# Second layer's sums through two wide buffers, attention's weights prepared earlier, last output block by block

## The reference, cut to what matters

```python
xn = layernorm(x)                                   # over the last axis
def rfs(v):                                         # 256 random features
    return exp(xis) / 16 * exp(v @ (xis[:, None] * proj).T - 0.5 * sum(v * v) * xis**2)
s = rfs(xn) @ rfs(input_weights).T                  # 256 features, 256 outputs
h = silu(xn @ w1.T * w1_s) * (xn @ w2.T * w2_s)     # 256 -> 1024
h = gelu(h @ h1.T * h1_s)                           # 1024 -> 1024
h = gelu(h @ h2.T * h2_s)                           # 1024 -> 1024
out = x + s * silu(h @ w3.T * w3_s)                 # 1024 -> 256
```

## Time and profile before

| | us |
|---|---|
| median of 3 runs | 1387.88 (1386.78 to 1389.29) |
| the profiled execution's own time | 1389.23 |
| its span, first to last instruction | 1387.4 |
| PE busy | 1328.2 (96%) |
| DVE busy | 963.5 (69%) |
| ACT busy | 784.9 (57%) |
| POOL busy | 595.2 (43%) |
| DMA, mean rate over the span | 140 GB/s |

### The profile page before, as it was taken

One profiled execution on the slowest core, in us unless ns is written; L12 is line 12 of the kernel. 1 busy time (PEld: TensorE's weight loads), 2 busy tenths in 40 slices (PEclk: granted clock), 3 DMA queues, 4 the chain that ended last, 5 costly groups with the idle time before them and its releaser, 6 DMA issues.

```text
span 1387.4 us, 17297 instructions
## 1 busy us (share of the span) xinstructions
PE 1328.2 (96%) x6684; PEld 1133.9 (82%) x6684; DVE 963.5 (69%) x1233; ACT 784.9 (57%) x1065; POOL 595.2 (43%) x624
## 2 busy tenths in 40 slices
PE   5999099999999999999999999999999999999996
PEld 4888089888888889888898888988888888988886
DVE  6677086787977787688866777566776666666574
ACT  4556065566655656555655566555665565655663
POOL 4545598889888888899982000000000000000000
PEclk9999599999999999999999999999999999999999
DMA  9975443254522554234432444224442244313441
GB/s 363 336 269 195 133 150 99 96 175 160 167 95 87 168 171 130 99 126 160 163 109 70 152 139 140 89 74 137 152 137 77 76 138 151 107 46 122 138 150 48
DMA packets 88647, 193.89 MB, mean 140 GB/s; under 512 B 10608, under 2 KB 12400, under 8 KB 87920
## 3 DMA queue, kind: packets, MB, share of 16 engines
q1 hardware_dynamic: 79088, 160.22, 34.7%
q0 software_dynamic: 9472, 32.51, 6.8%
HBM read 167.53 MB, written 34.60 MB: 146 GB/s over the span
## 4 chain that ended last, share of the span: by engine, by line
PE 86%; DMA 7%; POOL 5%; issue 1%; DVE 0%; SPq 0%; ACT 0%; POOLq 0%; DVEq 0%
PE ps L205 67%; PE ps L208 18%; DMA ry<-in_h 4%; POOL ry L490 3%; DMA hs<-ry 1%; PE ps L220 1%; DMA s<-in_h 1%; DMA quad<-in_w 1%; POOL quad L490 1%; POOL hs L80 0%; POOL ry L80 0%; POOL s L490 0%; DVE ry L188 0%; DMA ry<-in_x 0%; DMA ring<-hs 0%
## 5 line engine op out<-in xcount | busy, mean ns | idle before, releaser
L205 PE MATMUL ps<-split,ring 128*128 128x512 f32 x2800 | 764.8, 390 | 31.7 <-DMA ring<-hs 31.7
L205 PEld LDWEIGHTS ps<-split,ring 128*128 128x128 f32 x2800 | 526.2, 188 | 141.9 <-DMA ring<-hs 32.8
L188 DVE TENSOR_TENSOR split<-quad,split 128x1024 fp32r<-128x1024 f32 x256 | 330.3, 1300 | 179.5 <-ACT split L184 179.1
L184 ACT ACTIVATE split<-quad 128x1024 fp32r<-128x1024 f32 x256 | 266.0, 1052 | 88.3 <-PE ps L208 70.6
L208 PE MATMUL ps<-split,ring 128*128 128x512 f32 x784 | 305.2, 389 | 0.0
L205 PE MATMUL ps<-xT,w 128*128 128x512 f32 x768 | 219.5, 394 | 4.7 <-DVE xT L188 2.5
L527 POOL TENSOR_TENSOR cube<-cube,seen 128x256 f32<-128x256 f32 x176 | 190.7, 1084 | 13.8
L184 ACT ACTIVATE quad<-quad,cols 128x512 f32<-128x512 f32 (+1 forms) x194 | 138.9, 718 | 91.9 <-DVE quad L188 91.8
L184 ACT ACTIVATE quad<-ps 128x512 f32<-128x512 f32 x192 | 112.5, 596 | 135.0 <-PE ps L208 134.9
L205 PEld LDWEIGHTS ps<-xT,w 128*128 128x128 f32 x768 | 145.1, 190 | 35.2 <-DVE xT L188 2.9
L208 PEld LDWEIGHTS ps<-split,ring 128*128 128x128 f32 x784 | 147.3, 188 | 30.6
(11 more groups left out here) (94 smaller groups left out, 1160.9 us busy)
## 6 DMA issues: line engine op xcount, KB each, us to landing
ring<-hs SPq DMA_DIRECT2D x448, 256.0 KB, 3.4
xin<-in_x SPq DMA_DIRECT2D x16, 512.0 KB, 5.5
s_h<-s SPq DMA_DIRECT2D x16, 512.0 KB, 2.9
seen<-in_h POOLq DMA_DIRECT2D x64, 128.0 KB, 2.9
ry<-in_x SPq DMA_DIRECT2D x16, 512.0 KB, 4.6
out<-ry SPq DMA_DIRECT2D x16, 512.0 KB, 2.7
...
```

The costliest lines, as they stand in the source:

```text
L184: return act.mark(lambda e: e.activation(dst, src, func, scale=scale))
L188: return dve.mark(lambda e: e.tensor_tensor(dst, a, b, op))
L205: pe.run(lambda e: e.matmul(dst, stat, mov, start=start, stop=stop, skip_group_check=loose))
```

## The change

**The factory in two parts.** The second layer's sums are taken out of `factory` and put into `factory_second`. `qrow` and `stage` become one tensor `rows` (128 x 4 x 512), and the second layer's k-parts go through `ry` and `rows`, whole, four rounds instead of eight. POOL waits for the last user of `qrow` and `stage` first, the dots of h1 of the first tile. The loads stand ahead of `copy_raw`, which was ahead of them. In the first layer, `load(3)` moves behind `make(2)`.

The diff, cut to its core:

```diff
+    def close(self):
+        self.todo = self.closing
...
         value = engine.value_load(flag)
+        for make in self.closing:
+            make(engine)
         with engine.If(value > 0):
...
-            qrow = [sf(f"qrow{j}", [P, T]) for j in range(2)]
-            stage = [sf(f"stage{i}", [P, T]) for i in range(2)]
+            rows = sf("rows", [P, 4, T])
...
+            pe.wait(*free[banks[0]], *free[banks[1]])
+            turned = [None] * KD
+            for b in range(NB):
+                pe.wait(xn_done[h, b])
+                for kd in range(KD):
+                    def one(e, b=b, kd=kd):
+                        return e.transpose(ps[:, banks[kd], b * P:(b + 1) * P], xin[j][:, b, kd * P:(kd + 1) * P], ident[:, :])
+                    turned[kd] = pe.mark(one) if b == NB - 1 else pe.run(one)
+            tok = turned[-1]
             for kd in range(KD):
-                pe.wait(xn_done[h], *free[banks[kd]])
-                tok = turn(ps[:, banks[kd], :], xin[j], kd)
-                hi = cast(xT[j][:, kd, 0, :], ps[:, banks[kd], :], tok, *xT_free.get(h - 2, []))
+                hi = cast(xT[j][:, kd, 0, :], ps[:, banks[kd], :], turned[kd], *xT_free.get(h - 2, []))
                 xT_lo[h] = vv(xT[j][:, kd, 1, :], ps[:, banks[kd], :], xT[j][:, kd, 0, :].bitcast(F32), ALU.subtract, hi)
...
+        d_pj.send(sp, pj, proj.rearrange("(a p) d -> p a d", p=P))
+        d_wi.send(sp, wi, win.rearrange("(a p) d -> p a d", p=P))
         lands = {}
         for half in range(2):
             for n, name in enumerate(("w1", "w2")):
                 lands[n, half] = quad[(1, 4)[n]][:, 2 * half:2 * half + 2, :]
                 d_w12[2 * n + half].send(sp, lands[n, half], w_kpm[name][:, :, half * T:(half + 1) * T])
         load_x(1)
-        d_pj.send(sp, pj, proj.rearrange("(a p) d -> p a d", p=P))
-        d_wi.send(sp, wi, win.rearrange("(a p) d -> p a d", p=P))
...
-            bufs = wide + [quad[0][:, :, :], res, yt]
-            use = [0, 1, 2, 1] + Q * [3, 4]
-            todo = [(0, k, 0, T) for k in range(Q)] + [(1, k, c, T // 2) for k in range(Q) for c in (0, T // 2)]
+            bufs = wide + [quad[0][:, :, :], rows[:, :, :]]
+            use = [0, 1, 2, 1, 1, 3, 1, 3]
+            todo = [(layer, k) for layer in range(2) for k in range(Q)]
             landed = {}
             def load(n):
-                layer, k, c, width = todo[n]
+                layer, k = todo[n]
                 v = wT[("h1", "h2")[layer]].rearrange("(j k p) (i c) -> k p j i c", j=2, p=P, i=2)[k]
-                before = stored[1 if n in (4, 5) else use[n]]
-                if before.count:
-                    pool.wait(before.token)
+                if stored[use[n]].count:
+                    pool.wait(stored[use[n]].token)
                 for j in range(2):
-                    landed[n] = d_land[use[n]].send(pool, bufs[use[n]][:, 2 * j:2 * j + 2, :], v[:, j, :, c:c + width])
+                    landed[n] = d_land[use[n]].send(pool, bufs[use[n]][:, 2 * j:2 * j + 2, :], v[:, j, :, :])
...
-                tok = stored[use[n]].send(pool, hs[layer][k][:, Q:2 * Q, c:c + width], bufs[use[n]])
-                piece_stored.setdefault((layer, k, 2), []).append(tok)
+                piece_stored[layer, k, 2] = [stored[use[n]].send(pool, hs[layer][k][:, Q:2 * Q, :], bufs[use[n]])]
...
-            for n in range(len(todo)):
+            for n in range(Q):
                 make(n)
-                if n == 1:
+                if n == 2:
                     load(3)
-                if n == 3:
-                    copy_raw(pool, 1)
-                    load(4)
-                    load(5)
-                if 5 <= n < len(todo) - 1:
-                    load(n + 1)
-            s_free[0][:] = s_free[1][:] = [stored[0].token]
-            yt_free[:] = res_free[:] = [stored[3].token, stored[4].token]
-            quad_free[0] = [stored[2].token]
+            return load, make
+        def factory_second():
+            pool.wait(*qrow_free[0], *qrow_free[1], *stage_free[0], *stage_free[1])
+            load, make = factory_rest
+            load(5)
+            load(4)
+            copy_raw(pool, 1)
+            make(4)
+            make(5)
+            load(6)
+            load(7)
+            make(6)
+            make(7)
+            stage_free[0] = stage_free[1] = qrow_free[0] = qrow_free[1] = [stored[3].token]
+            yt_free[:] = res_free[:] = [stored[1].token]
...
+        factory_rest = factory()
+        s_free[0][:] = s_free[1][:] = [stored[0].token]
+        quad_free[0] = [stored[2].token]
...
-        for half in range(2):
+        def round_w(half):
             for n, w in enumerate((w1, w2)):
                 w_round[n, half] = cast(w[:, :, half * T:(half + 1) * T], lands[n, half], d_w12[2 * n + half].token)
-        quad_free[1] = quad_free[4] = [w_round[1, 1]]
-        for task in stats_tasks([0]):
-            task()
-        pe.wait(c_ident)
-        turn_rows(0, (0, 1))
...
-            pe.wait(made_w["pj"], *free[0])
+            pe.wait(made_w["pj"])
             for kd in range(KD):
-                tok = turn(ps[:, 0, kd * R:(kd + 1) * R], pj, kd, KD)
-            two = ps[:, 0, :].rearrange("p (a b) -> p a b", a=2)
+                tok = turn(ps[:, 2, kd * R:(kd + 1) * R], pj, kd, KD)
+            two = ps[:, 2, :].rearrange("p (a b) -> p a b", a=2)
             hi = cast(PT[:, 0, :, :], two, tok)
-            made_w["PT"] = vv(PT[:, 1, :, :], two, PT[:, 0, :, :].bitcast(F32), ALU.subtract, hi)
-            free[0] = [made_w["PT"]]
+            def rest():
+                made_w["PT"] = vv(PT[:, 1, :, :], two, PT[:, 0, :, :].bitcast(F32), ALU.subtract, hi)
+                free[2] = [made_w["PT"]]
+            return rest
...
+        def exponents_win():
             for r in range(KD):
-                made_w["ex", r] = vst(WF[:, r, :], qw, ab2[:, r:r + 1], ps[:, 1, r * D:(r + 1) * D], ALU.mult, ALU.add,
-                                      tok, made_w["q"], made_w["a2"], made_w["sq"])
-            free[1] = [made_w["ex", r]]
+                made_w["ex", r] = vst(WF[:, r, :], qw, ab2[:, r:r + 1], ps[:, 0, r * D:(r + 1) * D], ALU.mult, ALU.add,
+                                      made_w["dots"], made_w["q"], made_w["a2"], made_w["sq"])
+            free[0] = [made_w["ex", r]]
...
+        ORDER_END = [("b22", 1, 1), ("b12", 1, 0), ("b11", 0, 0), ("b21", 0, 1)]
+        def y_place(h, b):
+            if h == 2 * NT - 2:
+                return (0, 1, 4, 5)[b], 0
+            return 2 * (h % 2) + b // 2, (b % 2) * D
         def down(t, C, between):
+            order = ORDER if t + 1 < NT else ORDER_END
+            use = {"b11": 2, "b22": C.slot, "b12": 1 - C.slot}
+            use["b21"] = use[order[0][0]]
+            for g in range(2):
+                C.split("b12", g, use["b12"])
+            quad_free[C.at["b12"]] = [C.ready["b12"]]
             begun = set()
-            use = [2, C.slot, 1 - C.slot, 2]
-            for n, (name, j, kq) in enumerate(ORDER):
-                slot = slots[use[n]]
+            for n, (name, j, kq) in enumerate(order):
+                slot = slots[use[name]]
                 pe.wait(C.ready[name], d_w3.token)
                 last = j in begun
                 for b in range(NB):
-                    bank = 2 * j + b // 2
+                    bank, col = y_place(2 * t + j, b)
                     pe.wait(*free[bank])
                     terms = [(slot[:, k, g, b * P:(b + 1) * P], w3[:, Q * kq + k, :]) for k in range(Q) for g in range(2)]
-                    tok = group(ps[:, bank, (b % 2) * D:(b % 2 + 1) * D], terms, not last and b % 2 == 0, last, True)
-                    if last and b % 2:
-                        y_done[2 * t + j, b // 2] = tok
+                    tok = group(ps[:, bank, col:col + D], terms, not last and col == 0, last, True)
+                    if last:
...
-                if n < 2:
-                    nxt = ORDER[n + 2][0]
+                slot_free[use[name]][:] = [tok]
+                if n == 0:
                     for g in range(2):
-                        C.split(nxt, g, use[n + 2])
-                    quad_free[C.at[nxt]] = [C.ready[nxt]]
+                        C.split("b21", g, use["b21"])
+                    quad_free[C.at["b21"]] = [C.ready["b21"]]
...
+        pe.wait(c_ident)
+        scale_proj()
+        rest_proj = turn_proj()
+        rest_win = turn_win()
+        round_w(0)
+        for task in stats_tasks([0]):
+            task()
+        rest_proj()
+        rest_win()
+        turn_rows(0, (4, 5))
+        dots_win()
+        norms_win()
+        round_w(1)
+        quad_free[1] = quad_free[4] = [w_round[1, 1]]
...
-                side[1].append(scale_proj)
-                side[2].append(lambda: turn_norms(0, 0))
-                side[4].append(turn_proj)
-                side[5].append(turn_win)
+                side[1].append(turn_norms_win)
+                side[2].append(exponents_win)
```

(29 more changed lines are left out.)

50 lines of the change are left out of this document (24 added, 26 removed).

## The result

The changed kernel takes 1353.15 us, median of four runs (1351.36 to 1355.45), beside 1388.43 for the kernel before on the same chip (four runs, 1386.78 to 1389.29). The ratio is 0.9748, with a 95% interval of 0.9727 to 0.977: faster by 35.3 us. The profiled execution took 1351.43, with a span of 1349.6 us against 1387.4.

A forecast was written before the change was run, and what follows sets the result against it. TensorE's matmuls bound seven tiles of eight; in the first, POOL's second-layer sums stall TensorE. Terms -34.4 + 4 - 2.6 - 5.4 = -38.4 us take 1389.23 to 1350.8, less 1.35 for the median: 1349.5; range 1343 to 1359.

The forecast's parts named there:

- the hole: First tile, second layer's product S2: TensorE waits for ring parts made from POOL's late sums; closing it gains 34.4 us.
- start, to the first product: First tile's start: attention weights' work moved ahead of the gated steps, those ending 0.4 earlier; -2.6 us, between +1 and -5.
- ring in the copy's shade: First tile's S1: weight parts land late beside the raw copy; 2.5 us wait plus 1.5 for the clock, +4 (0 to 8).
- b12's low part and the clock there: Last products: b12's low part is ready at 1363.88, where b12 could start at 1363.6; +0.3 us.
- last matmul to the span's end: Program end: last output by blocks, x loaded early, shorter store, flag read during the store; -5.7 us.
- a tie: Second layer's sums: last ring part lands at 140.5 us, TensorE wants it at 139.5; between 20 early and 10 late.
- the rival without a shade: First tile's ring parts are not slowed by the raw copy: no wait, POOL's chain faster, 1345.5 us; chance 0.20.
- The second case: Ring parts pass one packet of the raw copy and land nearly as in quiet: 1345.5 us; chance 0.20.
- the start gives nothing: Rival at the start: dots_win keeps TensorE 2 us beyond the split rows, DVE ends later: 1352.5 us; chance 0.05.
- The median of the runs lies 1.35 under it: Whole kernel: step from the profiled execution's forecast, 1350.8 us, to the runs' median, 1349.5 us.
- the hole moved to A11: Rival: second layer's copied quarters land after 115 us, so TensorE's wait moves to product A11: 1375 to 1388; chance 0.02.
- a wait for b21's split: Rival, seven tiles: b21's split before the rows' casts delays the next first gated step: 1390 and more; chance 0.02.

The follow-up runs named there:

- no_copy: The changed kernel without the second layer's raw copy, its raw quarters read from the first layer's copies (output not the reference's): 1343.62 us, ratio 0.9697.
- tail: The changed kernel with block b+1 scaled before block b is gated in the last output, additions of blocks 0 to 2 on POOL: 1358.46 us.
- hold: The changed kernel with one more wait: POOL's first addition starts only when VectorE has its rstd of rows 512 to 1023: 1351.41 us.
- whole_end: hold with the last half's Silu, gate, addition and store in one piece each instead of by blocks: 1352.2 us.

## Why the prediction was right, and where its steps failed

The sum for the profiled execution was -38.4 us; its span fell by 37.8. By the medians it was 35.3 instead of 38.4, so 1349.5 against 1353.15, inside the range. What carries the change, the hole, was read right, by mechanism and by size. That the rest came so near is luck: two terms were off by 5 to 7 us, each outside the bounds that the prediction gave it, and they cancelled:

| term | predicted | measured, by the traces |
| --- | --- | --- |
| hole | -34.4 | -34.4 |
| start, to the first product | -2.6 (+1 to -5) | -9.5 |
| to product 2 (the mix) | 0 | +0.5 |
| ring in the copy's shade | +4 (0 to 8) | +9.5; 8.4 of it gone in `no_copy` |
| b12's low part and the clock there | +0.3 | +0.4 |
| last matmul to the span's end | -5.7 | -4.2 |

**The hole.** Right, and with more in hand than "a tie": the last store was to land at 137 and the ring part at 140.5, and the store landed at 131.1. The loads took 6.4 and 7.3 us, not 10; a round 6.8 to 7.1 and not 8; and the first store landed in 13.7 from 87.45, at 101.2, not 107. What started the chain was not the end of the features, though: the first load went out at 65.87, right behind a store, and the second, with the copy behind it, at 70.78, when the store of the first layer's last sums has landed. That store is late because its load, moved behind `make(2)`, kept POOL waiting 13.42 us. With the load moved back (`load3_early`) POOL does wait for the features, to 65.19. All the same the chain had some 5 us in hand at its end (131.1 and a ring part's 3.6 against 140).

**The ring.** The mechanism was right and was shown by taking the copy away, and the rival without a shade fell. The step that failed is "get 10 us or more", with "the fourth, at the spacing that half the DMA rate gives": S1's parts took 12.2 and S3's 13.5. S1 waited 4.4 instead of 2.5, S3 waited too (1.52, not in the sum), and the clock's share was not 1.5 but some 3.2 in S1, which took 14.83 us from 85.75 to 100.58 instead of 7.26. A price of 10.1 us, read beside the copy and loads of the kernel before, was used for another mix of queues, and the clock's share was taken from a wait half as long. The second case, that a ring part would "pass one packet of the copy and land nearly as in quiet", did not come: 12.2 and 13.5 us against 4.4 and 3.3.

**The start.** That "its work until the second half's rows is the same within 0.1 us" is the step that failed, where the prediction has DVE set the pace. The operations are the same, but their place against POOL's first addition is not, and with it their time. In the trace of the kernel before most of them lay behind its start (21.39). With the new start their end lies within half a microsecond of it, and the side on which it falls is worth 5 to 6 us at the first product; 3.2 of them were left at the tile's end in `tail`. In the slow order the first product starts at 61.1 to 61.7, 3.5 to 4.0 us ahead of 65.15 and near the forecast. In the quick one, 0.95 of the 9.5 us is there at the first gated step (13.52), 4.9 in all when the second half's rows are turned (30.55 for 35.48), 2.2 are the work taken away, and the other 2.4 are TensorE's pace: the granted clock of 30 to 40 us was 0.79 before and is 1.00 now. A smaller difference between executions lies ahead of that: the first seven matmuls of `dots_win` take 1.07 us in the changed kernel's trace and 1.83 in `hold`'s, whose first gated step starts at 15.10, as forecast. What decides this is open. The case "the start gives nothing" is out.

**The median.** "The median of the runs lies 1.35 under it" was carried from the kernel before. For the changed kernel the profiled execution was one of the two quick ones, and the median lies 1.7 above it. The kernel before has its median 0.8 under its profiled execution by the four runs of the result. These two make the 2.5 us between 37.8 and 35.3, and the sum's own error is the other 0.6.

**The end.** Size near (4.2 for 5.7), reason wrong. The 4.0 was worked out from the chain by blocks, but `whole_end` has nearly the same end without blocks, 0.4 us later behind TensorE's last matmul (8.1 for 7.7 in `hold`). The shorter store and the flag's reading beside it, priced at 1.4 together, gave 0.5: the last addition's end lies 3.64 us ahead of the span's end, 4.15 before. The other two rivals, the hole moved to A11 and a wait for b21's split, did not come: tiles one to seven cost the same in both traces within 0.4 us.
